# Attention on one core: the weighted sum of odd key chunks given as one piece of sixteen matmuls, of even chunks as two pieces of eight

## The reference

```
HQ, HKV = (32, 8); HD = D // HQ       # 16 features a head, 4 query heads share a key head
Q, K = _rope(Q, K)
scores = einsum('bhqd,bhkd->bhqk', Q, K) / sqrt(HD)
w = softmax(scores, axis=-1)
attn = einsum('bhqk,bhkd->bhqd', w, V)
```

## Time and profile before

| | us |
|---|---|
| Median of 3 runs | 3103.22 (3099.01 to 3103.26) |
| The profiled execution | 3101.82 |
| Its span, first to last instruction | 3100.0 |
| Attention proper in that span | about 1041.8 to 2264 |

### The profile page before, as it was taken

How to read it: one execution, slowest core, us unless ns; L and a number is a source line. 1 busy time by engine, 2 the same in 40 slices (tenths; PEclk the granted TensorE clock), 3 DMA queues, 4 the chain that set the end, 5 groups by cost and what they waited for, 6 DMA issues and landing times. The chain is left out here.

```text
span 3100.0 us, 61305 instructions
## 1 busy us (share of the span) xinstructions
PE 2967.1 (96%) x20310; PEld 1183.7 (38%) x20310; DVE 1867.4 (60%) x2221; ACT 1739.7 (56%) x3220; POOL 795.3 (26%) x772
## 2 busy tenths in 40 slices
PE   7889999999998999999999999999997999999999
PEld 4434444444564122222222222222233444444444
DVE  6852222221676999999999999999723222222221
ACT  5643333333111499999999999999910333333332
POOL 0144444444443000000000000000022444444444
PEclk9999999999999799999999999999989999999999
DMA  4311110011333011111111111111356011111100
GB/s 130 110 52 41 41 39 16 27 41 42 91 104 104 10 33 31 31 31 31 31 31 30 30 30 31 31 30 30 101 166 226 13 41 41 41 41 41 41 14 28
DMA packets 163904, 160.58 MB, mean 52 GB/s; under 512 B 62552, under 2 KB 100824, under 8 KB 163808
## 3 DMA queue, kind: packets, MB, share of 16 engines
q1 hardware_dynamic: 163808, 159.30, 17.8%
HBM read 111.48 MB, written 47.19 MB: 51 GB/s over the span
## 5 line engine op out<-in xcount | busy, mean ns | idle before, releaser
L1780 DVE TENSOR_REDUCE at_neg_max<-at_max_ps 128x1 f32<-128x1024 f32 x1024 | 1174.4, 1217 | 39.7 <-PE at_max_ps L1636 38.8
L1763 ACT ACTIVATE at_probs<-at_score_ps 128x512 f32<-128x512 f32 x2048 | 1116.7, 597 | 75.4 <-PE at_score_ps L1656 46.4
L1636 PE MATMUL at_max_ps<-at_km,at_q 48*128 48x512 f16 x2048 | 634.7, 390 | 19.1 <-DVE at_neg_max L1780 8.8
L1656 PE MATMUL at_score_ps<-at_q,at_ks 50*128 50x512 f16 x2048 | 627.5, 384 | 24.5 <-DMA at_q<-at_max_parts 19.5
L1665 PE MATMUL at_out_ps<-at_probs,at_v 128*32 128x256 f32 x8192 | 644.7, 393 | 3.4
L983 DVE SCALAR_TENSOR_TENSOR f_h<-f_up_ps,hr_factor,f_gate 128x512 f32<-128x512 f32 x128 | 96.1, 751 | 475.3 <-ACT f_gate L1057 473.2
L1725 POOL CAST at_max_parts<-at_max_rows 16x128 f16<-16x128 f32 x64 | 17.9, 280 | 1182.8 <-ACT at_max_rows L1736 1182.8
L413 DVE SCALAR_TENSOR_TENSOR f_h<-f_up_ps,hr_factor,f_gate 128x512 f32<-128x512 f32 x112 | 83.9, 749 | 393.4 <-PE f_up_ps L752 240.0
L1665 PEld LDWEIGHTS at_out_ps<-at_probs,at_v 128*32 128x32 f32 x8192 | 169.1, 109 | 394.8 <-issue 211.7
L1656 PEld LDWEIGHTS at_score_ps<-at_q,at_ks 50*128 50x128 f16 x2048 | 132.2, 94 | 448.1 <-ACT at_probs L1763 396.1
L1057 ACT ACTIVATE f_gate<-f_gate_ps 128x512 f32<-128x512 f32 x128 | 76.4, 597 | 353.0 <-PE f_up_ps L1130 353.0
(11 more groups left out here) (149 smaller groups left out, 3738.3 us busy)
## 6 DMA issues: line engine op xcount, KB each, us to landing
rows<-x SPq DMA_DIRECT2D x40, 1024.0 KB, 5.6
x<-rows SPq DMA_DIRECT2D x16, 1024.0 KB, 4.6
f_raw<-units SPq DMA_DIRECT2D x48, 256.0 KB, 2.7
at_q<-qk_parts SPq DMA_DIRECT2D x384, 32.0 KB, 1.8
rows<-x SPq DMA_DIRECT2D x32, 256.0 KB, 2.8
at_q<-at_max_parts SPq DMA_DIRECT2D x512, 1.0 KB
att<-at_out SPq DMA_DIRECT2D x256, 32.0 KB
out<-rows SPq DMA_DIRECT2D x8, 1024.0 KB, 4.2
```

Of the source, the lines that this page charges most:

```text
L1636: done = nc.tensor.matmul(max_ps[u % 2][:, half * QB:(half + 1) * QB], q[k][rows, j // SLOTS, h * QB + c * P:h * QB + (c + 1) * P], km[k][ ...
L1656: nc.tensor.matmul(score_ps[pos % RING][:], ks[k][rows, kc * P:(kc + 1) * P], q[k][rows, j // SLOTS, h * QB:(h + 1) * QB], start=True, sto ...
L1763: nc.scalar.activation(probs[:, kc % PBUF, j, :], score_ps[pos % RING][:], ACT.Exp, scale=HD ** -0.5).then_inc(exps, 1)
L1780: nc.vector.tensor_reduce(neg_max[:, h, column:column + 1], max_ps[u % 2][:], AX.X, ALU.max, negate=True).then_inc(maxed, 1)
```

## The change

In chunks 3, 5 and 7 of each pass the piece after `i` = 1 is taken out, and both pieces stand after `i` = 3. Chunks 2, 4, 6 (and 0 and 1) stay as they were.

```diff
@@ -1710,8 +1710,11 @@
                                 pe.wait_ge(out_copied, n + 1)
                                 weigh(n, k, 0, 0)
                                 weigh(n, k, 0, 1)
-                            elif kc >= 2:
+                            elif kc >= 2 and kc % 2 == 0:
                                 weigh(n, k, kc - 1, i // 2)
+                            elif kc >= 2 and i == 3:
+                                weigh(n, k, kc - 1, 0)
+                                weigh(n, k, kc - 1, 1)
```

## The result

The changed kernel takes 3110.79 us (median of 7, 3109.9 to 3116.64), the kernel before 3101.12, measured beside it (median of 7, 3098.13 to 3103.26). The ratio is 1.0035, 95% interval 1.0024 to 1.0047: slower by 0.35%, some 10 us, and the interval does not reach 1. The forecast was 3115, in a range of 3099 to 3130.

What follows compares the result with a forecast made beforehand. TensorE was taken to bound odd passes, SyncE's DMA queue even ones. Losses of 8.1 us over 14 sets of four passes and 4.6 less half a microsecond over eight others, about 12 us, gave 3115 us, range 3099 to 3130.

Steps and rivals of the forecast that it cites:

- The ring's chain: Chunks 3, 5, 7: fourth score waits for ScalarE to free its bank of three; chunk 2.40 us instead of 2.21.
- rival A: Merged chunks: the ring is no wait, the saved switch is real; 20 us gained, 3083 us; chance 0.08.
- VectorE's wait beside it: Merged chunks: second block of maxima waits for VectorE to free its buffer; claimed covered by 0.08 us, getting no later.
- Rival C: Chunk's second half: VectorE binds, or the piece of sixteen starts 0.1 us later; x = 0.3, 3138 us; chance 0.15.
- The pass: TensorE's own time in each pass grows by 3 x 0.19 = 0.57 us from the merged chunks.
- the 0.1 at chunk 1: Pass 26's kind: a wait for VectorE at chunk 1 may give 0.1 us back, as VectorE is no longer behind.
- a term that I had counted for pass 27 only: Pass 27's kind: without the DMA wait its third score comes 1.11 us after the first, not 1.23; 0.12 gained.
- What the even passes give back: SyncE's DMA chain gets 0.44 us more lead; pass 24's kind gains 0.36 us, pass 26's loses 0.02.
- VectorE's idle time: In the attention, VectorE's idle time should rise from 39.7 us by about 12.

Runs made afterwards that it cites:

- the run with chunk 7 alone: Kernel before with only chunk 7's two pieces merged, chunks 3 and 5 keeping two pieces: 3099.39 us, ratio 0.9991 to the kernel before.
- The two runs with the stores first: SyncE issues the eight stores of split maxima ahead of the six km loads: kernel before with this 3081.0 us, changed kernel with this 3113.29 us.
- the run with both taken away: Changed kernel, split-maxima stores ahead of km loads, exponentials over 64 of 512 columns, reductions over 512 of 1024: 2990.72 us; kernel before with the same: 3022.53 us.

## Why the prediction was right

- **The ring's chain.** 1.08 us from first to fourth score was forecast, 1.07 measured; 0.31 to the piece, 0.32 measured; 1.01 to the next score, 1.01 measured. The chunk of 2.40 us was put together from four rows of different places, and holds. In this the sum was right, and rival A (no wait, 3083 us) failed at the condition it named.
- **VectorE's wait beside it.** Forecast as covered by 0.08 us, and no later in the pass. In chunk 3 the cover is 0.26 us from maxima to score, less the 0.22 that the second half needs: 0.04. In chunks 5 and 7 it is gone: the wait ends 0.06 us later there, so "no later" was wrong, at a price of 0.01 us a chunk. In the run with chunk 7 alone it failed, at 0.34 us instead of 0.19, and I had forecast that run with 0.19. Rival C's mechanism is real; in this kernel it costs next to nothing.
- **The pass.** Passes 25 and 26 take 19.02 us; 19.14 (18.57 + 0.57) and 19.02 (19.12 less the 0.1 at chunk 1) were forecast. Up to chunk 3 a pass has become 0.13 us shorter (1452.90 - 1445.52 = 7.38, before 7.51), in pass 26's kind as forecast, as VectorE is no longer behind, and in pass 25's kind because no DMA wait precedes it, a term that I had counted for pass 27 only.
- **What the even passes give back.** Pass 24: 19.22 forecast, 19.15 measured, as it too became 0.06 us shorter up to chunk 3 (7.51 after, 7.57 before). The wait for DMAs was to vanish, and did. The two runs with the stores first size it: 22 us given back of 32.
- **The back edge of the loop.** Not forecast: ahead of pass 28, where TensorE's loop closes, the piece of sixteen is followed by a score only 1.19 us later, 0.18 more than elsewhere. Before, it was 0.03 more (a `weigh` at 1650.24, a score at 1650.85). It comes once in four passes, some 14 times, 2.5 us. That it is the loop's branch is a guess from its place; what takes the time, and why it was hidden before, no run tells.
- **Where luck helped.** Four passes lose 0.54 us, where 0.58 was forecast, because errors cancel: 0.12 us too much for pass 25 and 0.07 for pass 24, and 0.15 too little for pass 27, by the back edge.
- **VectorE's idle time.** Forecast to rise by 12 us, from 39.7. It fell to 36.3. This sign was wrong, and by the way of reading: reductions of 1.22 us start every 1.13 when nothing holds them, so they overlap, and a wait of up to 0.08 us shows as busy time. Busy rose by 1188.1 - 1174.4 = 13.7 us instead, for the same 1024 instructions. Counted by starts, the time beyond 1.13 us from one reduction to the next rose from 53 to 63 us in all. So 10 of the 12 us are there, and the idle column doesn't show them.

The forecast of 3115 is 4 us above what was measured. The sum was made of 12 us against 10 measured, so the rest is the median of the kernel before, which was 3101.1 beside the changed kernel and 3103.2 in the runs shown ahead of the prediction.

## What to carry to other kernels

Before you merge pieces of work to save a switch, count how many producers then stand in a row against the buffers they fill: with four scores on a ring of three banks, the fourth waits for a whole round of the consumer, here 0.42 us against the 0.23 saved. Look at what already waits at the same place, since a loss of 32 us showed as 10 where a queue of DMAs was late anyway, and the order of that queue was worth 20 us by itself. Where two waits are almost equally long, taking away one shows little (a merged chunk of 2.41 or 2.39 us for 2.40); only the run with both taken away told what the change was worth.

## What the runs showed of the hardware

- A switch from the matmuls of 64 rows to those of 32 columns and back costs TensorE some 0.2 us: 2.21 us a chunk with two round trips, 2.03 with one, at a granted clock of 1.00 and with the same matmuls. The Trainium skill (TensorEngine Tiling (Array Packing), Key Properties) says that a change of the tiling mode drains the array. The trace agrees that the switch costs time, and gives the size; that the drain is what costs it, no run shows by itself.
- A full exponential of 128 x 512 is 0.60 us long and one of 64 columns is 0.22, but either begins only 0.42 us after its score starts. So with 64 columns the ring's chain is still 0.70 us from first to fourth score (1407.99 - 1407.29).
